# Attention scores from two float32r parts in 32-row quarters of TensorE instead of three bfloat16 parts in 64-row halves

## What is computed

```python
def reference(x, ...):
    xn = _layernorm(x)
    q, k, v = jnp.split(xn @ Wqkv, 3, axis=-1)        # 16 heads of 8
    Q, K = _apply_rope(Q, cos, sin), _apply_rope(K, cos, sin)
    scores = jnp.einsum('bhqd,bhkd->bhqk', Q, K) / math.sqrt(Dh)
    scores = jnp.where(causal, scores, jnp.finfo(scores.dtype).min)
    y = jnp.einsum('bhqk,bhkd->bhqd', jax.nn.softmax(scores), V)
    return x + y @ Wproj + ffn(xn)                    # gate, up, down, and the experts
```

## Time and profile before

| | |
|---|---|
| median of 3 runs | 736.49 us (734.74 to 736.72) |
| span of the profiled execution | 737.5 us, 1.0 above that median |
| busy: PE, DVE, ACT, POOL | 658.8, 591.9, 539.6, 446.4 us |
| first product of scores that starts, last `mr` that ends | 47.34 and 679.83 us |

### The profile page before, as it was taken

One profiled execution on the slowest core, in us unless ns is written; L12 is line 12 of the kernel. 1 busy time (PEld: TensorE's weight loads), 2 busy tenths in 40 slices (PEclk: granted clock), 3 DMA queues, 4 the chain that ended last, 5 costly groups with the idle time before them and its releaser, 6 DMA issues. The chain is left out here.

```text
span 737.5 us, 15130 instructions
## 1 busy us (share of the span) xinstructions
PE 658.8 (89%) x5628; PEld 268.0 (36%) x5628; DVE 591.9 (80%) x1204; ACT 539.6 (73%) x833; POOL 446.4 (61%) x652
## 2 busy tenths in 40 slices
PE   3977787779999989999999979999998999999996
PEld 2433233223334433333234434433333333344343
DVE  4549898999989999896976898877999898855451
ACT  3333455777878676899887686788689999888882
POOL 5358525656486999953962758904277588601960
PEclk9999697998999999999999989999999999999999
DMA  6562521300000143031000043140001000010001
GB/s 145 103 127 49 73 36 24 47 14 3 2 14 20 54 74 61 15 71 20 1 10 21 17 80 63 21 76 13 2 14 31 4 14 1 16 32 16 8 15 38
DMA packets 36566, 26.67 MB, mean 36 GB/s; under 512 B 7084, under 2 KB 34092, under 8 KB 36492
## 3 DMA queue, kind: packets, MB, share of 16 engines
q1 hardware_dynamic: 35628, 24.92, 17.6%
q10 hardware_dynamic: 864, 0.79, 0.6%
HBM read 6.23 MB, written 2.10 MB: 11 GB/s over the span
## 5 line engine op out<-in xcount | busy, mean ns | idle before, releaser
L1159 DVE TENSOR_REDUCE pmax<-banks 128x2 f32<-128x1024 f32 (+3 forms) x304 | 342.2, 1160 | 55.6 <-PE banks L1331 36.3
L1006 ACT ACTIVATE pT<-banks 128x1024 f32<-128x1024 f32 (+3 forms) x384 | 295.8, 810 | 74.1 <-PE banks L1359 54.7
L1373 PE MATMUL ybank<-pT,vaug 128*32 128x512 f32 (+3 forms) x1536 | 164.7, 512 | 2.0 <-ACT pT L1006 1.3
L870 POOL TENSOR_TENSOR ssum<-sim 128x512 f32<-128x512 f32 x128 | 145.6, 1143 | 22.9 <-DVE wsum L1206 18.8
L1350 PE MATMUL banks<-qs,ks 51*128 51x512 bf16 (+3 forms) x768 | 123.2, 336 | 22.8 <-ACT pT L1006 14.1
L1321 PE MATMUL banks<-ks,qs 48*128 48x512 bf16 (+3 forms) x768 | 113.4, 337 | 25.5 <-DVE pmax L1159 16.2
L1206 DVE SCALAR_TENSOR_TENSOR wsum<-ssum,best,wsum 128x512 f32<-128x512 f32 x128 | 125.2, 992 | 11.8 <-ACT wsum L1052 11.7
L1052 ACT ACTIVATE wsum<-ssum,wbias 128x512 f32<-128x512 f32 x128 | 90.3, 723 | 24.4 <-POOL ssum L870 22.2
L887 POOL TENSOR_TENSOR coef<-coef,wsum 128x512 f32<-128x512 f32 x64 | 85.4, 1334 | 20.9 <-DVE wsum L1206 20.5
L1350 PEld LDWEIGHTS banks<-qs,ks 51*128 51x128 bf16 x768 | 36.8, 94 | 133.0 <-ACT pT L1006 78.3
L1321 PEld LDWEIGHTS banks<-ks,qs 48*128 48x128 bf16 x768 | 33.1, 94 | 121.6 <-DVE pmax L1159 62.3
(11 more groups left out here) (111 smaller groups left out, 783.8 us busy)
## 6 DMA issues: line engine op xcount, KB each, us to landing
qs<-parts SPq DMA_DIRECT2D x90, 64.0 KB
ks<-parts SPq DMA_DIRECT2D x90, 64.0 KB
xin<-in_L_attn_x SPq DMA_DIRECT2D x4, 512.0 KB, 5.4
osb<-in_L_attn_x SPq DMA_DIRECT2D x8, 256.0 KB, 2.8
yz<-yT SPq DMA_DIRECT2D x64, 32.0 KB
yz<-yT SPq DMA_DIRECT2D x32, 64.0 KB
out<-osb SPq DMA_DIRECT2D x8, 256.0 KB, 3.2
qs<-negmaxT SPq DMA_DIRECT2D x32, 12.0 KB
```

What stands on the lines that cost most here:

```text
L870: g.tensor_tensor(ssum[:, m % NSS, :, :], s[:, h, 0:XI].unsqueeze(2).to_broadcast([P, XI, NKEYS]), s[:, RH + h:RH + h + 1, :].to_broadcast ...
L1006: a_.activation(pT[:, q % NPT, 2 * e:2 * e + 2, q0:CHUNK], pair(("sc", *n))[:, :, q0:CHUNK], ACT.Exp, scale=SCALE).then_inc(out_sem, 1)
L1159: v.tensor_reduce(pmax[:, c, i % TPC, k0 // CHUNK, js[0] // PP, :, js[0] % PP:js[-1] % PP + 1], pair(("mx", b, c, k))[:, :, 0:wd_ * len(js ...
L1373: ins = t_.matmul(ybank[32 * j:32 * j + 32, q0:CHUNK], vaug[:, b % 2, kt, v0:v0 + 32], pT[:, q % NPT, j, q0:CHUNK], start=kt == 0, stop=kt ...
```

## The change

Two parts in place of three: `high`, the number rounded by ACT to float32r, and the rest, kept as float32 and read by TensorE as float32r. TERMS has three products, 24 rows (26 with the two rows of the maximum), so a head fits into a 32-row quarter. A task still makes the scores of two heads, now in two quarters: `half` 0 uses quarters 0 and 1, `half` 1 uses 2 and 3. Two tasks of different half may be written with "+" in PE_ORDER; their products and mask steps are then issued in turn. 79 pairs of tasks are written so. Masks take four steps, of 32, 64, 96 and 128 columns, in each of two quarters: 8 products for a task on the diagonal where there were 4. The program's matrix products go from 5628 to 7356. `c1`, `v2` and `p2` are gone, `n1` has two operations instead of four, `nr` has four DMAs of 8 KB instead of two of 12 KB, the DMAs of `ga` are still twelve a unit of 64 KB. `rp` waits for the DMAs of the unit before the last. All five tables are written anew.

```diff
-TERMS = [(0, 0), (0, 1), (1, 0), (0, 2), (1, 1), (2, 0)]
+TERMS = [(0, 0), (0, 1), (1, 0)]
 KQ = len(TERMS) * DH
-KE = KQ + 3
+KE = KQ + 2
...
-            units += [(i, k0, w, range(j, j + n)) for j in range(0, PAIRS, n)]
+            units += [(i, k0, w, range(j, j + n), half) for j in range(0, GROUPS, n) for half in range(2)]
...
-sc.0.0.1.1.0@45 pv.0.0.1.0 mx.0.1.15@23 sc.0.0.1.1.1@45 mx.0.1.16@01 mx.0.1.17@23 sc.0.0.1.2.0@45 pv.0.0.1.1
+sc.2.1.0.4.1@45+sc.2.1.0.4.0@23 mx.2.1.49@01 pv.2.1.0.3 mx.2.1.50@45 sm.2.7@6 sc.2.1.0.5.0@23+sc.2.1.0.5.1@01
...
                     for t, term in enumerate(TERMS):
-                        for hh in range(2 if m > 0 else 1):
-                            r = HALF * hh + DH * t
+                        for e in range(NE if m > 0 else NE // 2):
+                            r = ROWS * e + DH * t
                             dst = ks[r:r + DH, b % 2, :, cols] if a else qs[r:r + DH, m % NQS, :, :]
-                            sp.dma_start(dst, parts[HALF * hh:HALF * (hh + 1), u % 2, term[a], :])\
+                            src = high[:, u % 2, :].bitcast(F32) if term[a] == 0 else tAB[:, u % 2, 1, :]
+                            sp.dma_start(dst.bitcast(F32), src[ROWS * e:ROWS * (e + 1), :])\
                                 .then_inc(rows_loaded[u % 2], 16)
...
-                    g.tensor_tensor(tAB[:, s, 0, :], tAB[:, s, 0, :], parts[:, s, 0, :], ALU.subtract)\
-                        .then_inc(out_sem, 1)
-                elif kind == "p2":
...
-                    g.tensor_tensor(parts[:, s, 2, :], tAB[:, s, 0, :], parts[:, s, 1, :], ALU.subtract)\
+                    g.tensor_tensor(tAB[:, s, 1, :], tAB[:, s, 0, :], high[:, s, :].bitcast(F32), ALU.subtract)\
                         .then_inc(out_sem, 1)
...
-                    a_.activation(parts[:, s, int(kind == "c1"), :], tAB[:, s, 0, :], ACT.Copy).then_inc(out_sem, 1)
+                    a_.activation(high[:, s, :], tAB[:, s, 0, :], ACT.Copy).then_inc(out_sem, 1)
...
-                    if u >= 4:
-                        w.wait_ge(done["p2"], rank("p2", *unit_at(u - 2)))
-                    elif u >= 2:
-                        w.wait_ge(done["v2"], rank("v2", *unit_at(u - 2)))
+                    if u >= 2:
+                        w.wait_ge(rows_loaded[a], rows(*unit_at(u - 2)))
...
+            def quarter_masked(task, h):
...
+                    gr, kt, half = n
+                    q0 = first_column(c, kt)
+                    m = ROWS * (h + 1)
+                    for e in range(2):
+                        r = slice(ROWS * (2 * half + e), ROWS * (2 * half + e + 1))
+                        ins = t_.matmul(pair(task)[:, e, q0:q0 + m], shifted[r, P - m:2 * P - m],
+                                        maskT[r, P - m:P], start=False, stop=h == NE - 1,
+                                        tile_position=(r.start, 0))
...
+            def scores(task):
...
+                for e in range(2):
+                    q = ROWS * (2 * half + e)
+                    r = slice(q, q + KE)
+                    ins = t_.matmul(pair(task)[:, e, q0:CHUNK], ks[r, b % 2, gr, kt * P:(kt + 1) * P],
+                                    qs[r, serial(b, c) % NQS, gr, q0:CHUNK], start=True, stop=kt < c * TPC,
+                                    tile_position=(q, 0))
...
+                elif kind in ("mx", "sc"):
+                    if task not in PARTNER.values():
+                        together = [t for t in (task, PARTNER.get(task)) if t]
+                        for t in together:
+                            scores(t)
+                        for h in range(NE):
+                            for t in together:
+                                if diagonal(t):
+                                    quarter_masked(t, h)
```

More of the change, by code:

```diff
@@ L7 @@
 BF16 = mybir.dt.bfloat16
+F32R = mybir.dt.float32r
 ALU = mybir.AluOpType
@@ L52, in max_units @@
             n = max(1, CHUNK // w)
[L53 removed]
+            units += [(i, k0, w, range(j, j + n), half) for j in range(0, GROUPS, n) for half in range(2)]
     return sorted(units, key=lambda u: u[3][0] // PP)
 MAX_UNITS = [max_units(c) for c in range(NC)]
[L58 removed]
+LAST_UNIT = [[max(k for k, u in enumerate(units) if u[3][0] // PP <= h) for h in range(PARTS)] for units in MAX_UNITS]
@@ L61, in parse @@
 def parse(text):
-    order, place = [], {}
+    order, place, partner = [], {}, {}
     for word in text.split():
-        name, _, slot = word.partition("@")
-        kind, *rest = name.split(".")
-        task = (kind, *(int(r) for r in rest))
-        order.append(task)
-        if slot:
-            place[task] = [int(k) for k in slot]
-    return order, place
-PE_ORDER = """
-rt.0@01 rt.1@23 xt.0@01 qk.0.0.0@01 qk.0.0.1@23 su.0@01 su.1@45 gt.0.0.1@6 vm.0@01 su.2@23 qk.0.1.0@45 gt.0.0.2@6
@@ L206 @@
-sc.3.0.3.1.1@01 sc.3.0.3.2.0@23 ac.3.1.7 sc.3.0.3.2.1@01 pv.3.0.3.0 pv.3.0.3.1 pv.3.0.3.2 sc.3.0.3.3.0@01
-sc.3.0.3.3.1@23 ac.3.1.8 pv.3.0.3.3 dn.3.0.2@5 dn.3.0.3@6 dn.3.0.1@4 ot.3.1@3 dn.3.0.0@5 ct.3.0.1@6 ct.3.0.2@4
-ct.3.0.0@5 ct.3.0.3@3 ac.3.0.0@6 ac.3.0.1 ac.3.0.2 ac.3.0.3 ac.3.0.4 ac.3.0.5 ac.3.0.6 ac.3.0.7 ac.3.0.8 ot.3.0@6
+        together = []
+        for part in word.split("+"):
+            name, _, slot = part.partition("@")
+            kind, *rest = name.split(".")
+            task = (kind, *(int(r) for r in rest))
+            together.append(task)
+            if slot:
+                place[task] = [int(k) for k in slot]
@@ new lines, in parse @@
+        order += together
+        if len(together) == 2:
+            partner[together[0]] = together[1]
+    return order, place, partner
+PE_ORDER = """
+rt.1@01 rt.0@23 xt.0@45 su.1@23 su.0@45 qk.0.0.0@01 qk.0.0.1@45 gt.0.0.1@6 gt.0.0.2@1 vm.0@45 up.0.0.1@6 up.0.0.2@1
+qk.0.1.0@23 gt.0.0.3@6 su.2@01 up.0.0.3@6 gt.0.0.0@3 dn.0.0.2@5 qk.0.1.1@01 sm.0.0@6 sm.0.1@4 up.0.0.0@2 dn.0.0.0@3
+dn.0.0.1@6 xt.1@01 mx.0.0.0@45 mx.0.0.1@23 mx.0.0.2@01 sm.0.2@6 qk.1.0.0@45 dn.0.0.3@6 mx.0.0.3@01+mx.0.0.4@23
@@ L966, in _ @@
                     w.wait_ge(first_loaded, 16 * NFIRST)
-                    for e in range(2):
+                    for e in range(NE):
                         ins = a_.activation(rope_wide[:, NT * s + 4 * i:NT * s + 4 * i + 4, e, :, :],
                                             rope_sb[:, s, 4 * i:4 * i + 4, :].unsqueeze(3)
-                                            .to_broadcast([P, 4, DH, PAIRS]), ACT.Copy)
+                                            .to_broadcast([P, 4, DH, GROUPS]), ACT.Copy)
                     ins.then_inc(out_sem, 1)
-                elif kind in ("c0", "c1"):
+                elif kind == "c0":
                     b, c, a = n
@@ L1246, in _ @@
                 out_sem = done[kind]
-                if task in BEFORE:
-                    for t in BEFORE[task]:
-                        w.wait_ge(done[EMPTIED_BY[t[0]]], RANK[emptier(t)])
+                if kind not in ("mx", "sc"):
+                    emptied(task)
                 if kind == "su":
```

861 lines of the change are left out of this document (430 added, 431 removed), and 5 rows, old and new, of the table KINDS.

## The result

The changed kernel takes 876.91 us (871.27 to 879.79, 4 runs) against 735.89 of the kernel before: 1.191 times as long, with a 95% interval of 1.186 to 1.196. The forecast was 732.6 with a range that ended at 772. Ahead of everything else stands the clock. The page of the changed kernel: its span, busy time by engine, and the clock that TensorE was granted in 40 slices, in tenths.

The account below looks back on a forecast made before the run. PE was taken to set the pace in 0.60 of the 631.7 us between first and last score maximum, DVE in the rest. Terms summed to -3.9 on a 737.5 us span, giving 733.6; runs lie 1.0 lower: 732.6 us, range 706 to 772.

Parts of the forecast that it names:

- Weight loads: PE, float32r loads in the open where a run of score products begins, 278 runs: +13 us, between nothing and 26.
- The rival on loads: PE: float32r weights load at 189 ns, in the open at runs and behind masks; 746 to 762 us, chance 0.25.
- The other two rivals: PE: float32r streams at half rate (790 to 860 us, chance 0.09); quarters don't run side by side (over 860, 0.04).
- Pairs: PE: 79 pairs written with "+" run side by side, 28.2 us instead of 46.0, -17.9.
- Masks: PE, diagonal tasks: four mask steps take 0.133 us where two took 0.080, at most +27.3 us over 432 tasks.
- the bound of +8: PE: mask steps of 32 columns shorter than their weight load, 432 times 0.02 us at most, kept for the range.
- The end: Behind the last maximum: fewer PE products and a chain moved to the middle, -8 us, between -4.8 and -12.7.
- the neighbours: PE: 83 off-diagonal tasks followed by one of the other half overlap like pairs, -16.4 us, or -8.2 if half wait.
- The order: DVE: twelve kp moved from behind the last maximum into the middle, +4 us, between 0 and 13.2.
- The start: Before the first score product: no c1 and v2 (-1.3 us), DMAs in larger pieces (-2.6), together -4.
- The wait of `rp`: DVE at the start: the fourth unit's rp now waits for the first keys, +1.2 us, nothing if DVE finds holes.
- the pieces of the DMAs: Query and key DMAs at the start in pieces of 2 KB instead of 1 KB: -2.6 us, between 0 and -10.5.

Follow-up runs that it names:

- e3: The kernel before with three products of parts instead of six, so 24 and 27 rows in each half instead of 48 and 51: 826.05 us, ratio 1.122.
- e4: The kernel before with its 48 and 51 rows, but the third part made zero, so 24 rows hold products with zero: 735.00 us, ratio 0.998.
- e6: The changed kernel with six rows of zeros added in each quarter by memsets, 30 and 32 rows instead of 24 and 26: 860.71 us.
- e7: The changed kernel with bfloat16 parts instead of float32r and six rows of zeros per quarter, 30 and 32 rows: 776.44 us.
- e1: The changed kernel with its two parts in bfloat16 instead of float32r, same quarters, pairs and order: 791.34 us, ratio 1.076.
- e9: The kernel before with two bfloat16 parts, zeros keeping 48 and 51 rows, and the changed kernel's five tables, pairs not joined: 774.11 us, ratio 1.054.
- e8: The kernel before in its halves and order with two bfloat16 parts, without c1, v2 and p2, zeros keeping 48 and 51 rows: 733.75 us, ratio 0.997.
- e2: The changed kernel with each "+" in PE's table replaced by a space, so 79 pairs run one task after the other: 892.28 us.

## Why the prediction was wrong

**The clock had no term.** Every product was priced at 2.4 GHz from rows where the clock was full, and the sum was made as if the clock stayed where it was. The earlier trace rows showed a clock of 0.93 in a stretch with waits, and I did not ask what it hung on. The change halves the rows that a score product puts to work, from 48 and 51 of each 64-row half to 24 and 26 of two 32-row quarters. That alone is 91 us in the kernel before (e3 against e4), and up to 114 of the 136 us here are clock. Three things have a part in it. With few rows the clock stays low for longer each time (10 stretches of 23 us on average in e3, against 8 of 6.0 before; more rows gave clock back in e6 and e7). With float32r, its loads in the open or its products, it does so too (13.2 us on average with it, 9.6 without, e1; a clock of 0.842 and 0.884). The written order makes it fall more often (15 times in e9 against 8 in e8; 0.940 against 0.974). How they add in one kernel stays open, and so does what the chip counts. The masks, which now use 32 rows where they used 64, were not tested apart.

**Weight loads: right place, wrong size.** The term was 278 runs of score products times 0.047 us, +13, at most +26. A float32r load is in the open at every product behind one on the same rows, not only at the start of a run, for 0.11 us each (two neighbours on different halves pay it once); without float32r, 38 us of span x clock were gone, some 4 of them by the earlier start. The rival on loads had the right mechanism, and nearly the size: it named the loads behind masks, though its sum still counted only the 278 runs, and 735 us of span x clock at the clock of the kernel before would be some 760 us (an estimate: 735/0.968), inside its 746 to 762. The 877 are the clock, which it did not have either. The Trainium skill ("TensorE: Matmul & The Clock Gate", "Weight-path perf modes") says that the fast weight load is for 128 weights of types other than FP32. The loads of float32r behave here as if it counted as FP32 (208 ns against 93 for the same load in bfloat16). The Trainium skill ("TensorE: Matmul & The Clock Gate", Part 3) also says that a load overlaps with products under way only when its row group differs. That fits float32r here, whose product starts 0.113 us behind one of 128 columns on the same rows and 0.01 us behind one on others (700.69 and 700.70). It does not fit the bfloat16 masks, whose loads start with the product ahead of them on the same rows.

**The other two rivals fell.** float32r streams about one column at 2.4 GHz (0.057 us for 128), not half that, and quarters run side by side (700.69 and 700.70).

**What held.** Pairs: -17.9 us of PE forecast, which the sum counted at 0.60, so -10.7; e2 measured 15.4 us at a clock of 0.83, 8 of them in span x clock. Masks: the four steps take 0.15 to 0.17 us (447.38 to 447.64 less a switch of 0.09 to 0.11), not 0.133; the first, of 32 columns, takes 0.04, and the bound of +8 was for this. The end: from the last maximum 50.20 us instead of 57.70, -7.5 where I took -8. In all, e1, which has the quarters, pairs, masks and order but no float32r loads, is 17 us less than the kernel before in span x clock; the sum without its load term was -12 (-3.9 less 13 x 0.60). That is close partly by luck: some 5 of the 17 are a first product that float32r's DMAs do not allow (42.72 us, against 47.34 before), and the neighbours came to half.

**What did not.** The neighbours: the term of -16.4 was taken whole, but only 41 of the 83 tasks start within 0.05 us of the one ahead in the changed kernel; the others wait for operands or banks. That is the lower bound, -8.2, by count; no run measured it by itself. The order: taken at +4 for its `kp`, it cost 12 us of span x clock in halves (e9); what it costs in quarters is not shown. The start: the first product came at 47.19, not 43. It no longer waits for the DMAs itself; that wait now sits ahead of an `rp`. PE, and under it DVE, between 35 and 37 us of the changed kernel (in brackets the wait ahead):

```profile
36.70 1.86 PE L1421 MATMUL banks<-xnT,wg_sb 128*128 128x512 f32 x2 [2.50 <-DVE tAB L1138]
```

```profile
35.42 1.22 DVE L1138 TENSOR_TENSOR tAB<-banks,cs 128x1024 f32<-128x1024 f32 x1 [3.73 <-DMA qs<-tAB]
```

The wait of `rp` for the DMAs of the unit before the last, for which I had put 1.2 us on the fourth unit, holds DVE for 3.73 us at the third; PE waits 2.50 for the banks that this `rp` empties. From 36.70 on PE works without a wait, in part at the lower clock, through the products that the new table has put ahead of the first `mx`. In e1, whose DMAs have half the bytes, that `rp` came at 32.64 instead of 35.42 and the first product at 42.72. So the 1.3 us of `c1` and `v2` and the pieces of the DMAs, together -4 in the sum, came to -0.2.

## What to carry to other kernels

Before packing more, smaller products into TensorE, look at the granted clock, at how long it stays low after each wait, and at how many rows each product uses. A product that does its arithmetic in half the rows can make the whole kernel slower, though its columns cost the same; rows of zeros gave the clock back here. Price a new number format by the distance between starts on the chip, load and product together, for every product, and not only where a run of them begins. And compare runs of different clocks by span times clock as well, so that work and clock are told apart, as far as TensorE is waited for.
